# One-hot tiles for the token lists: seven short two-scalar instructions in place of two long ones

## The reference

```python
logits = xt @ Wr + br
probs = jax.nn.softmax(logits, axis=-1)
top_p, top_idx = jax.lax.top_k(probs, TOP_K)          # TOP_K = 2 of E = 8 experts
weights = top_p / top_p.sum(axis=-1, keepdims=True)
...
h = gelu(einsum('end,edh->enh', xe, W1) + b1)         # for every expert e
y = einsum('enh,ehd->end', h, W2) + b2
out = (weights[:, :, None] * take(y, top_idx)).sum(axis=1)
```

## Time and profile before

| | us |
|---|---|
| median of three runs | 1970.54 (1970.01 to 1972.72) |
| the profiled execution | 1971.19 |
| its span, first to last instruction | 1969.4 |
| mean granted TensorE clock | 0.941 |

### The profile page before, as it was taken

How to read it: one execution, slowest core, us unless ns; L and a number is a source line. 1 busy time by engine, 2 the same in 40 slices (tenths; PEclk the granted TensorE clock), 3 DMA queues, 4 the chain that set the end, 5 groups by cost and what they waited for, 6 DMA issues and landing times.

```text
span 1969.4 us, 36324 instructions
## 1 busy us (share of the span) xinstructions
PE 1734.1 (88%) x10852; PEld 1222.6 (62%) x10852; DVE 1438.8 (73%) x3115; ACT 1080.1 (55%) x2380; POOL 1219.4 (62%) x1150
## 2 busy tenths in 40 slices
PE   7769899999999989989898987644999999999997
PEld 5535555555555545555455554543889898989996
DVE  7777777868788777787877878798666666666664
ACT  5656666656666665666666663662444434343443
POOL 1277777777777777777777774102366565556553
PEclk9979999989999999999999989775999999999999
DMA  5554446455465455654546452387132333333322
GB/s 169 167 151 129 136 140 164 129 142 157 138 167 142 134 147 140 165 141 134 148 139 165 121 136 65 117 290 208 31 53 47 53 47 53 48 52 49 51 42 34
DMA packets 142680, 233.52 MB, mean 119 GB/s; under 512 B 31127, under 2 KB 107553, under 8 KB 141313
## 3 DMA queue, kind: packets, MB, share of 16 engines
q0 software_dynamic: 62800, 147.54, 31.4%
q1 hardware_dynamic: 69765, 81.13, 13.5%
q10 hardware_dynamic: 9932, 2.52, 0.7%
HBM read 188.81 MB, written 43.15 MB: 118 GB/s over the span
## 4 chain that ended last, share of the span: by engine, by line
PE 49%; DVE 16%; POOL 14%; issue 10%; DMA 7%; ACT 2%; DVEq 1%; ACTq 0%; POOLq 0%; SPq 0%
PE bank L1940 14%; POOL gather_ring L1061 14%; PE bank L1957 14%; PE bank L1185 8%; PE bank L1150 6%; DVE acc L1079 4%; DMA gather_ring<-node_table,src_slot 3%; DVE gather_ring L1106 2%; DMA w_stage<-in_L_ffn_W 2%; PE bank L930 2%; PE bank L1161 1%; PE bank L1921 1%; PE bank L678 1%; DVE w_lo L953 1%; ACT r_ring L1330 1%
## 5 line engine op out<-in xcount | busy, mean ns | idle before, releaser
L1061 POOL DMA_INDIRECT gather_ring<-node_table,src_slot x879 | 846.0, 962 | 268.0 <-issue 254.3
L1185 PE MATMUL bank<-gather_ring,onehot 128*128 128x264 f32 x1758 | 479.0, 409 | 91.4 <-DVE acc L1079 87.6
L1079 DVE TENSOR_TENSOR acc<-acc,bank 128x264 f32 x879 | 377.2, 429 | 194.6 <-DVE acc L1079 103.4
L1185 PEld LDWEIGHTS bank<-gather_ring,onehot 128*128 128x128 f32 x1758 | 315.8, 192 | 242.0 <-DVE acc L1079 189.8
L1150 PE MATMUL bank<-ones 128*128 128x512 bf16 x1760 | 421.9, 395 | 0.0
L2024 POOL DMA_INDIRECT out_rows<-y,token_idx x105 | 201.4, 1918 | 221.7 <-DMA out_rows<-y,token_idx 151.1
L1150 PEld LDWEIGHTS bank<-ones 128*128 128x128 bf16 x1760 | 170.3, 101 | 200.8 <-issue 32.6
L1992 ACT ACTIVATE hid<-bank,cols 128x256 f32<-128x256 f32 (+1 forms) x448 | 210.3, 551 | 141.5 <-PE bank L1940 138.6
L1940 PE MATMUL bank<-xe,w_hi 128*128 128x256 f16 (+1 forms) x1792 | 284.7, 267 | 0.9 <-ACT hid L1992 0.5
L1957 PE MATMUL bank<-w,hid_hi 128*128 x1680 | 278.3, 273 | 0.1
L1206 ACT ACTIVATE onehot<-iota_free,neg_dst 128x128 f32<-128x128 f32 x880 | 267.3, 386 | 0.0
(11 more groups left out here) (286 smaller groups left out, 2023.3 us busy)
## 6 DMA issues: line engine op xcount, KB each, us to landing
w_stage<-in_L_ffn_W SPq DMA_DIRECT2D x16, 1024.0 KB, 5.5
dst_row<-dst_rows SPq DMA_DIRECT2D x110, 128.0 KB
gather_ring<-node_table,src_slot POOLq DMA_INDIRECT x879, 2.8
w_split<-w_out SPq DMA_DIRECT2D x32, 256.0 KB, 3.0
w<-w_split SPq DMA_DIRECT2D x8, 1024.0 KB, 13.0
node_table<-acc SPq DMA_DIRECT2D x24, 264.0 KB
xt<-in_x SPq DMA_DIRECT2D x24, 256.0 KB, 3.0
r_ring<-in_x SPq DMA_DIRECT2D x6, 896.0 KB, 10.6
```

The costliest lines, as they stand in the source:

```text
L1061: e.indirect_dma_start(out=gather_ring[:, b % GB, j, :], out_offset=None, in_=node_table, in_offset=bass.IndirectOffsetOnAxis(ap=src_slot[ ...
L1079: e.tensor_tensor(a, a, bank[AGG[s % len(AGG)]][:, 0:ROW].rearrange("p (a c) -> p a c", a=1), ALU.add).then_inc(added, 1)
L1185: e.matmul(bank[AGG[s % len(AGG)]][:, 0:ROW], onehot[:, b % OHB, j, :], gather_ring[:, b % GB, j, :], start=True, stop=True).then_inc(summ ...
```

## The change

`tile_hot` now has the node tile outside and the 105 tiles innermost, and it is written by seven instructions in a round, one for each node tile. Each compares `iota_tile`, now a single row of 105 numbers, with the node's tile number and multiplies by the token, both taken as a scalar per partition. `lane_hot` is made first and is what it was. The wait between the instructions of a round goes, since none reads another's result. The tile numbers and the tokens are kept in f32 in place of f16. The matmuls read `tile_hot` without a step.

```diff
-        tile_hot = hot.take("tile_hot", [P, 2, FT, 7], F16)
+        tile_hot = hot.take("tile_hot", [P, 2, 7, FT], F16)
...
-        iota_tile = tail.take("iota_tile", [P, FT, NG], F16)
+        iota_tile = tail.take("iota_tile", [P, FT], F16)
...
-        tok16 = tail.take("tok16", [P, NT], F16)
+        tok_value = tail.take("tok_value", [P, NT])
...
-        spot16 = tail.take("spot16", [P, 2, 2, NT], F16)
+        spot_lane = tail.take("spot_lane", [P, 2, NT], F16)
+        spot_tile = tail.take("spot_tile", [P, 2, NT])
...
-            iota(iota_tile[:, :, :], [[1, FT], [0, NG]], 0, 0)
+            iota(iota_tile[:, :], [[1, FT]], 0, 0)
...
-                vector_order.of(e.tensor_tensor(tile_hot[:, i % 2, :, :], iota_tile[:, :, :],
-                                                for_hot(spot16[:, 1, c, tiles(g)], FT), ALU.is_equal))
-                vector_order.of(e.tensor_tensor(lane_hot[:, i % 2, :, :], iota_lane[:, :, :],
-                                                for_hot(spot16[:, 0, c, tiles(g)], P), ALU.is_equal))
-                e.wait_ge(vector_order.sem, vector_order.n)
-                e.tensor_tensor(tile_hot[:, i % 2, :, :], tile_hot[:, i % 2, :, :], for_hot(tok16[:, tiles(g)], FT),
-                                ALU.mult).then_inc(hots_made, 1)
+                e.tensor_tensor(lane_hot[:, i % 2, :, :], iota_lane[:, :, :],
+                                spot_lane[:, c, tiles(g)].rearrange("p (a n) -> p a n", a=1).broadcast_to([P, P, NG]),
+                                ALU.is_equal)
+                for j, n in enumerate(range(g * NG, (g + 1) * NG)):
+                    made = e.tensor_scalar(tile_hot[:, i % 2, j, :], iota_tile[:, :], spot_tile[:, c, n:n + 1],
+                                           tok_value[:, n:n + 1], ALU.is_equal, ALU.mult)
+                made.then_inc(hots_made, 1)
...
-                    made = e.matmul(bank[LIST][:, b * FT:(b + 1) * FT], lane_hot[:, i % 2, :, j], tile_hot[:, i % 2, :, j],
+                    made = e.matmul(bank[LIST][:, b * FT:(b + 1) * FT], lane_hot[:, i % 2, :, j], tile_hot[:, i % 2, j, :],
```

More of the change, by code:

```diff
@@ L1371, in vector_norm @@
             chain(e, e.tensor_scalar(below[:, :], iota_free[:, :], part[:, 0:1], None, ALU.is_gt))
-            e.tensor_tensor(tok16[:, :], tok_in_block[:, 0:NT], valid[:, :], ALU.mult).then_inc(below_made, 1)
+            e.tensor_tensor(tok_value[:, :], tok_in_block[:, 0:NT], valid[:, :], ALU.mult).then_inc(below_made, 1)
             e.wait_ge(sd_made, 1)
@@ L1620, in vector_route @@
             chain(e, e.tensor_single_scalar(spot_i[:, 1, :, :], spot_i[:, 0, :, :], 7, ALU.arith_shift_right))
-            vector_order.of(e.tensor_copy(spot16[:, 1, :, :], spot_i[:, 1, :, :]))
+            vector_order.of(e.tensor_copy(spot_tile[:, :, :], spot_i[:, 1, :, :]))
             chain(e, e.tensor_single_scalar(spot_i[:, 0, :, :], spot_i[:, 0, :, :], P - 1, ALU.bitwise_and))
-            chain(e, e.tensor_copy(spot16[:, 0, :, :], spot_i[:, 0, :, :]))
-            def for_hot(of, n):
-                return of.rearrange("p (a n) -> p a n", a=1).broadcast_to([P, n, NG])
+            chain(e, e.tensor_copy(spot_lane[:, :, :], spot_i[:, 0, :, :]))
             e.wait_ge(rows_stored[0], 16)
```

## The result

| kernel | us, median | runs | ratio to the kernel before |
|---|---|---|---|
| before | 1970.72 | 6 | |
| changed | 1977.34 (1975.85 to 1980.98) | 6 | 1.0032, 95% interval 1.0021 to 1.0043 |
| changed, second set | 1976.38 (1972.78 to 1980.02) | 11 | 1.0025, 95% interval 1.0016 to 1.0034 |

The kernel is slower, by 6.3 us in the first set (4.1 to 8.5) and by 4.9 us in the second (3.2 to 6.7, on a median of 1972.33 for the kernel before, 27 runs; the two medians themselves lie 4.05 apart). 1975.0 was forecast, 4.5 us more, on a base of 1970.54. The profiled execution of the changed kernel took 1975.85 us, its span is 1973.9, and that of the one before was 1969.4.

The account below looks back on a forecast made before the run. DVE was taken to bound the lists: 4.6 us more there, 0.1 less for matmuls, 0 for the clock, so +4.5 on 1970.54 gives 1975.0 us. Its own range was 1974.1 to 1976.6, the range with rivals 1972.4 to 1978.5.

Parts of the forecast that it names:

- the rival with slower elements: In the short DVE instructions, f16 elements go at the f32 rate (1977.4 us) or slower (1982.5); chance 0.20.
- DVE bounds the lists, and their growth is the kernel's: In the token lists, DVE's cost per round is paid fourteen times and everything behind moves as a block.
- (1): On DVE, the distance from start to start is an instruction's duration less 84 ns.
- (2): Fixed part of a short DVE instruction: 263 ns with two scalars, about 50 ns for each scalar.
- (3): Elements of a short DVE instruction: 0.30 ns for each f16 element, 31 ns for 105.
- The sum of the lists, 4.6 us: Fourteen rounds of 2.07 us in place of 1.74 make the lists 29.11 us against 24.50, 4.6 more.
- (4): PE's last seven matmuls read tile_hot without a step: 0 to 0.2 us saved, 0.1 taken.
- (5): At the experts' start, the shifted clock rise is worth -0.5 to +1.5 us; 0 taken.
- The rivals with hidden scalars: In the short DVE instructions, one scalar's fetch is hidden (1970.7 us, chance 0.15) or both are (1965.0, chance 0.05).
- both hidden, 1965.0: Neither scalar costs DVE time: a round of 1.35 us, the lists end 5.5 us earlier; chance 0.05.
- is anything late behind it?: Behind the lists, DMA queues are drained, and gathers, b2's load and the experts' first matmuls should move with the lists.

Follow-up runs that it names:

- wide128: The changed kernel with rows of 128 elements in place of 105, the matmuls reading the first 105; one execution, 1977.02 us, starts 223 ns apart.
- four_more: The changed kernel with four more such instructions in each round, writing to a spare tensor that nothing reads; 1.0086 of before, 17.0 us more.
- step7: The changed kernel with tile_hot in the old layout, written and read with a step of seven elements; one execution, 1984.95 us.
- no_scalar: The changed kernel with constants in place of both scalars per partition, so the lists hold no tokens; 0.9983 of before.
- one_scalar: The changed kernel with a constant in place of the tile number, the token still a scalar, lists without tokens; one execution, 1970.74 us.
- wait_one: The kernel before, with L1638 waiting for L1633 alone and no longer for L1635 too; 1969.19 us, 0.9986 of before.
- wait_one_w2_later: wait_one with the last four loads of w2 on SP's queue waiting until the stores of meta have landed; 0.9995 of before.

## Why the prediction was right, and where it was off

The sign, the size and the cause came out: slower, by 4.5 as forecast against 4.9 by the second set and by the profile's lists, and DVE's time for seven two-scalar instructions against two long ones is what did it. That the sum is so near is in part luck, since two of its terms are off in opposite directions. The median of the first set, 1977.34, lies above the forecast's own range (1974.1 to 1976.6) and on the price of the rival with slower elements, 1977.4; the profile and wide128 tell the two apart, the times do not. That of the second, 1976.38, lies in the range, on a base that had come out 1.8 us higher. Step by step:

- *DVE bounds the lists, and their growth is the kernel's.* Right. DVE stayed alone in the chain, and four_more returned 12.1 us for 12.2. The 16.4 us that PE sat idle say less than I took from them: 11.5 of them lie ahead of the first group, and a later round has 0.38.
- *(1) Start to start is the duration less 84 ns.* Right for these instructions (307 and 218: 89; 190 and 97: 93; 252 and 157: 95), but no law: step7 has 490 and 243.
- *(2) The fixed part, 263 ns for two scalars.* Too low. 307 less some 28 for 105 elements make about 280. Each scalar costs 62 and 55 ns, not 50. This is the term that was most mis-sized on DVE: 98 instructions at 8 ns more are 0.8 us.
- *(3) The elements, 31 ns.* Right: 23 by wide128's 0.22 ns for an element, 30 by no_scalar's 190 less 0.16 us. The rival of slower elements is out. The rule of the Trainium skill ("VectorE: DVE Perf Modes", section "The perf-mode tier table"), from which I estimated 27, agrees with the trace, at the odd length of 105 too.
- *The sum of the lists, 4.6 us.* It was 5.4 (29.90 less 24.50), a round of 2.125 where 2.07 was forecast.
- *(4) PE, 0.1 us.* It was 0.52. I had bounded the gain by the time of a load of weights, 0.132 us, as if that were its least distance; the matmuls follow each other at 0.089 while each load is shown with 0.153. This gain, 0.4 us larger than forecast, hides half of DVE's 0.8: 4.88 against 4.5, and that is the luck.
- *(5) The clock, 0.* The rise came after 2.02 us at the lower level and not 3.49, in the range given; with 592.2 against 593.2 us for the rest, 0.9 us came back in that execution, more than the 0.5 allowed for.
- *The rivals with hidden scalars.* Out by one_scalar and no_scalar. Their price was wrong as well: "both hidden, 1965.0" took 5.5 us off the lists and handed them to the end whole. no_scalar took more than that off the lists, and 3.4 us arrived.

The step that failed is therefore not in the forecast but in the sentence beside it: *is anything late behind it?* I read that the DMA queues had drained when the lists ended, and took it as room. It tells that a later list meets nothing. For an earlier one two things stand there. The first is the store of meta: where the first gather waited for it (wait_one, no_scalar, one_scalar), it started 28.6 to 31.4 us behind the lists' first instruction, and 28.9 before. By its last semaphore event the store landed between 26.9 and 31.8 us behind it in the kernels that left the loads of w2 and of b2 alone, so its room differs from one execution to the next. The second is the load of b2, issued just ahead of the fourth gather: that gather takes 5.1 us beside it, and 2.7 in no_scalar, where b2 had landed. A stretch can be worth a microsecond for each microsecond to the slow side and only a part of it to the fast side: half in no_scalar.

## What to carry to other kernels

Count a short DVE instruction by its fixed part and its scalars per partition before its elements: here 105 elements cost some 28 ns, the two scalars 117 and the rest some 162, so seven of them lost to two long instructions that did fourteen times 105 elements at a slower rate. Before a shortened stretch is credited with its whole gain, look for the other semaphores that the next engine waits on, and for what lands just ahead of the one that the profile names. Of a wait between instructions of one engine, ask which of them it really needs: letting L1638 wait for the instruction before last was the only edit here that kept the result and beat both kernels.

## What the runs showed that I had not expected

A matmul of 105 columns at the lower clock follows another after 0.089 us when its moving operand lies in one run, and after 0.167 with a step of seven f16 elements; the weights had the step in both. A DVE instruction that writes f16 with such a step is shown with 490 ns in place of 307, yet holds the engine for 25 ns more only. And the store of meta, 96 KB in pieces of 16 bytes, landed 32 us behind its issue beside the loads of w2 (wait_one, issued at 1331.97), and 23 us behind it without them (wait_one_w2_later, issued at 1333.69).
